# Delta rule in chunks: one TensorE product a level makes the inverse and its factor together, ScalarE copies both out, VectorE turns the factor from that copy

## The chip, the core and the metric

The kernel runs on one core of a Trainium2 chip, in one launch. The metric is the device time of an execution in microseconds (us). The engines are named as in the profile: PE is TensorE's matmul, PEld its weight load, DVE is VectorE, ACT is ScalarE, POOL is GpSimd, SP is SyncE. Each runs its own instructions in program order and waits for the others on semaphores.

## What is computed

The reference chains a gated delta rule, a mixture of experts, a linear attention and a softmax attention. Only the delta rule is touched (4096 tokens, 16 heads of 64):

```
def step(S, inp):
    q_t, k_t, v_t, g_t, b_t = inp
    Sk = einsum('bhkv,bhk->bhv', S, k_t)
    delta = einsum('bhv,bhk->bhkv', v_t, k_t) - einsum('bhv,bhk->bhkv', Sk, k_t)
    S = exp(g_t) * S + b_t * delta
    return (S, einsum('bhkv,bhk->bhv', S, q_t))
```

The kernel takes 64 tokens (a chunk) at once. Inside a chunk the updates depend on each other through a triangular matrix of 64 x 64 per head, which has to be inverted. The inverse is built by doubling: an inverse of blocks of 2, 4, 8, 16, 32 and at last 64.

## The kernel before

All 16 heads are worked on at once, as 8 pairs of heads side by side over 128 partitions; a tile of the phase (`W`) is 128 x 512, and a product over all heads is 16 `te.matmul` calls, which the trace shows as 32 matmul records. `SAME` products keep a head in its half of the array, `OTHER` products cross over, so that one of each can run side by side.

Two chunks (x = 0 and 1) make a couple, and there are 32 couples. `couples(one)` goes over them in 34 iterations. In each, every engine's `one(post, pre, ahead)` works on three couples: `ahead` gets its keys and the triangular matrix (`keys`, `take_upper` L1204, `minus_eye` L1366, `first_inverse` L1372), `pre` is inverted, and `post` goes through the state (`residual`, `updates`, `new_state`, `new_outputs`, `project`). 31 iterations have both `post` and `pre`. The order of the instructions in each engine is written by hand in `one`, the same in all iterations.

One level of the doubling, for each x, is a loop through three engines:

- TensorE `half`: the transposed inverse (`inv_low`) times the matrix (`upper`), into `pd_pre`.
- VectorE `mask_step` (L1250): `step` = `pd_pre` times a mask.
- TensorE `up`: `step` times `inv`, into `pd_low`, beside a product of `post`, `ahead` or the key rows.
- VectorE `turn_low` (L1259) transposes `pd_low` into `inv_low`; ScalarE `keep_inverse` (L1143) copies it to `inv`, with nobody waiting long for it.

There are five levels. Other instructions that matter below: on VectorE `turn_first` (L1255), `take_updates` (L1239), `take_state` (L1244), `turn_values` (L1219), `take_rows` (L1211). On ScalarE `grown` (L1122), `related` (L1127), `keep_values` (L1135, eight pieces of 32 x 256 per chunk), `keep_last_inverse` (L1149), `keep_outputs` (L1154). On GpSimd `decays` (L1334 and L1336), `grow_keys` (L1343), `grow_queries` (L1350), `decay_state` (L1355), `scale_rel` (L1361). ScalarE's `grown(pre, 1)` overwrites what `decay_state(post, 1)` on GpSimd reads, and so waits for it (`sdec_d`); `decay_state(post, 1)` reads the state that VectorE's `take_state(post, 0)` writes.

Lines 1796 to 2012 belong to the second norm phase, which the change doesn't touch. L852 is the line of the helper `product`, through which every 64 x 64 product goes.

## Time and profile before

| | us |
|---|---|
| median of 3 runs | 4261.81 (4256.46 to 4264.55) |
| profiled execution, its own time | 4283.9 |
| its span, first to last instruction | 4282.1 |
| delta phase, first key product to last projection | 541.3 to 1780.0 |
| PE busy | 3885.2 (91%) |
| DVE busy | 3064.9 (72%) |
| ACT busy | 2237.7 (52%) |
| POOL busy | 1036.7 (24%) |

The busy shares are over the whole program. The delta phase is 1239 us of it, and only there does the change act. Durations are those of single instructions; a matmul's end is modelled.

### The profile page before, as it was taken

Reading aid. Unit: us, or ns where it says so; the run is one execution under the profiler, and the core shown is the slowest. Engines: PE = TensorE matmul, PEld = TensorE weight load, DVE = VectorE, ACT = ScalarE, POOL = GpSimd, SP = SyncE. Lnnn points to the kernel's source line nnn. Section 1 sums busy time; section 2 is a strip of 40 time slices with the busy share of each in tenths; the row PEclk is TensorE's granted clock in tenths of the full one; section 3 lists DMA queues with packets and bytes.
Section 4 is the critical chain, followed back from the end, with each engine's and each line's share of the span. In section 5 each row is a group of like instructions: output and inputs, shape, how many; then the busy total and the mean of one; then the engine's idle time right before and its main releaser. Section 6 shows DMA issues by size and latency. Waiting matters only on the chain. (4 is left out here: it accounts for less than half of the span.)

```text
span 4282.1 us, 127123 instructions
## 1 busy us (share of the span) xinstructions
PE 3885.2 (91%) x51725; PEld 2324.9 (54%) x51725; DVE 3064.9 (72%) x5127; ACT 2237.7 (52%) x3389; POOL 1036.7 (24%) x1042
## 2 busy tenths in 40 slices
PE   5999778888888888897887999999999999999998
PEld 4444367777778777675663344444444444444443
DVE  5799856555555555444896787878878787878786
ACT  2788734444444444233442565656656565656564
POOL 1000055555555555102777000000000000000000
PEclk9999999999999999998896999999999999999999
DMA  3544432222222222224345000000000000000000
GB/s 126 183 124 124 142 116 81 84 79 89 85 83 79 85 82 83 75 86 142 106 110 121 8 5 19 5 8 15 10 15 10 13 5 20 5 20 3 10 15 10
DMA packets 271801, 265.25 MB, mean 62 GB/s; under 512 B 53760, under 2 KB 232064, under 8 KB 270496
## 3 DMA queue, kind: packets, MB, share of 16 engines
q1 hardware_dynamic: 250768, 226.07, 17.7%
q0 software_dynamic: 6144, 16.79, 1.2%
q10 hardware_dynamic: 14352, 14.55, 1.0%
q8 instruction: 420, 6.88, 0.7%
q14 instruction: 117, 0.96, 0.1%
HBM read 151.95 MB, written 105.38 MB: 60 GB/s over the span
## 5 line engine op out<-in xcount | busy, mean ns | idle before, releaser
L2418 DVE TENSOR_REDUCE part_max<-p_m 128x1 f32<-128x512 f32 x2118 | 1363.9, 686 | 378.1 <-PE p_m L2260 370.7
L2400 ACT ACTIVATE prob<-p_s 128x1024 f32<-128x1024 f32 x1024 | 1048.6, 1024 | 747.6 <-PE p_s L2324 745.6
L2279 PE MATMUL p_o<-prob,v_one 128*64 128x512 f32 x4096 | 1054.3, 592 | 3.9 <-ACT prob L2400 0.5
L2260 PE MATMUL p_m<-keys,queries 96*64 96x512 f16 x4236 | 661.4, 387 | 28.1 <-DMA keys<-parts_d 20.5
L2324 PE MATMUL p_s<-queries,keys 97*64 97x512 f16 x4096 | 619.0, 380 | 0.0
L2324 PEld LDWEIGHTS p_s<-queries,keys 97*64 97x64 f16 x4096 | 228.1, 109 | 598.4 <-issue 593.3
L2228 POOL TENSOR_TENSOR attn<-o_num,o_inv 32x512 f32<-32x512 f32 x64 | 81.2, 1268 | 1451.6 <-DVE o_inv L2437 1445.2
L852 PE MATMUL pd_pre<-inv_low,upper 64*64 64x64 f32 x10240 | 374.2, 222 | 45.3 <-issue 33.5
L2260 PEld LDWEIGHTS p_m<-keys,queries 96*64 96x64 f16 x4236 | 238.7, 108 | 311.1 <-DVE part_max L2418 56.5
L852 PE MATMUL pd_low<-inv,step 64*64 64x64 f32 x8192 | 365.1, 237 | 45.6 <-issue 42.2
L1143 ACT ACTIVATE inv<-pd_low 128x512 f32<-128x512 f32 x192 | 114.7, 598 | 519.1 <-DVE inv_low L1259 518.7
L2279 PEld LDWEIGHTS p_o<-prob,v_one 128*64 128x64 f32 x4096 | 287.7, 136 | 162.7 <-issue 15.9
L852 PEld LDWEIGHTS pd_pre<-inv_low,upper 64*64 64x64 f32 x10240 | 341.0, 137 | 59.9 <-issue 43.5
L852 PEld LDWEIGHTS pd_low<-inv,step 64*64 64x64 f32 x8192 | 326.9, 145 | 72.4 <-issue 69.9
L588 PE MATMUL p_proj<-xn_t_all,proj_w_sb 128*128 128x512 f32 x768 | 337.7, 596 | 7.7 <-PEq L2563 7.7
L1259 DVE STREAM_TRANSPOSE inv_low<-pd_low 128x512 f32<-128x512 f32 x256 | 183.2, 716 | 217.8 <-PE pd_low L852 214.9
L1250 DVE TENSOR_TENSOR step<-pd_pre,const 128x512 f32<-128x512 f32 x320 | 220.0, 688 | 94.0 <-PE pd_pre L852 73.5
L588 PEld LDWEIGHTS p_proj<-xn_t_all,proj_w_sb 128*128 128x128 f32 x768 | 146.8, 191 | 192.9 <-issue 187.7
L1135 ACT ACTIVATE v_row<-v_turned 32x256 f32<-32x256 f32 x512 | 211.9, 414 | 26.0 <-DVE v_turned L1219 19.1
L852 PE MATMUL pd_kq<-kq_t 64*64 64x128 f32 x2048 | 144.5, 295 | 35.1 <-DMA kq_t<-q_d 31.5
L852 PEld LDWEIGHTS pd_kq<-kq_t 64*64 64x64 f32 x2048 | 128.4, 148 | 37.2 <-issue 36.9
L2437 DVE RECIPROCAL o_inv<-o_raw 128x64 f32<-128x64 f32 x256 | 138.1, 542 | 0.0
(236 smaller groups left out, 5777.7 us busy)
## 6 DMA issues: line engine op xcount, KB each, us to landing
q_d<-conv_q SPq DMA_DIRECT2D x16, 1024.0 KB, 5.0
v_d<-conv_v SPq DMA_DIRECT2D x16, 1024.0 KB, 5.0
k_d<-conv_k SPq DMA_DIRECT2D x16, 1024.0 KB, 6.5
sums<-sums_d SPq DMA_DIRECT2D x128, 128.0 KB, 3.1
kq_t<-k_d SPq DMA_DIRECT2D x32, 512.0 KB, 3.7
kq_t<-q_d SPq DMA_DIRECT2D x32, 512.0 KB, 4.8
sums_k<-sums_d SPq DMA_DIRECT2D x128, 128.0 KB
v_t<-v_d SPq DMA_DIRECT2D x32, 512.0 KB
```

What stands on the lines that cost most here:

```text
L588: last = te.matmul(p_proj[u % RING][:], g.proj_w_sb[:, n, c, p * P:(p + 1) * P], g.xn_t[:, c, b * BLK:(b + 1) * BLK], start=c == 0, stop=c ...
L852: return te.matmul(out[half_of(h if to == SAME else 1 - h), p, :], lhs(p, half_of(h)), rhs(p, half_of(h)), start=start, stop=stop, skip_gr ...
L1135: last = a.activation(v_row[to_p, x, :, to_t], v_turned[from_p, :, from_t], ACT.Copy)
L1143: a.activation(inv_half[x][:] if k == NL - 1 else inv[x][:], p_low[x][:], ACT.Copy).then_inc(up_d[x], 1)
L1250: v.tensor_tensor(step[x][:], p_pre[x][:], over_pairs(masks[:, k - 1, :]), ALU.mult).then_inc(step_d[x], 1)
L1259: v.transpose(inv_low[x][:], p_low[x][:]).then_inc(lowc_d[x], 1)
L2260: last = te.matmul(p_m[k % 2][x * HALF:(x + 1) * HALF, :], queries[0:ROW, p, hh, at:at + HALF], keys[0:ROW, 2 * p + hh, kb * BLK:(kb + 1) ...
L2279: product = te.matmul(p_o[64 * hh:64 * hh + VW, :], g.v_one[:, j, p, hh:hh + 2, :].rearrange("p a d -> p (a d)"), prob[:, j % 2, hh, :], s ...
L2324: last = te.matmul(p_s[j % 2][x * HALF:(x + 1) * HALF, hh, :], keys[0:KR, 2 * p + hh, at:at + HALF], queries[0:KR, p, hh, :], start=True, ...
L2400: a.activation(prob[:, j % 2], p_s[j % 2][:], ACT.Exp, scale=SCORE_SCALE).then_inc(exp_d, 1)
L2418: v.tensor_reduce(part_max[:, hh * SUB + sub, kb:kb + 1], p_m[k % 2][:], AX.X, ALU.max).then_inc(red_d, 1)
L2437: v.reciprocal(o_inv[:, i * PW:(i + 1) * PW], o_raw[:, i * PW:(i + 1) * PW]).then_inc(inv_d, 1)
```

## The change

The matrix `upper` stays, but it is used once. `start_factor` multiplies the first transposed inverse with it: the result is a factor that already has the inverse in it. From there each level has one product of 128 columns: `step` times `both`, where `both` holds the factor in columns 0 to 63 and the inverse in columns 64 to 127 of each pair. ScalarE copies the 128 x 1024 result to SBUF (`keep_both`). VectorE transposes the factor half from that copy (`turn`) and masks the transposed tile (`mask`), which gives the next `step`. At the last level the masking is two small ScalarE copies into a tile with ones on its diagonal (`keep_half`, `last_step`). The key rows of x = 1 go through `pd_u` and into the next iteration, the products of `post` are put beside the long ones (each short product in the first half of a long one), and the order on every engine is written anew.

```diff
     p_both = [ps(f"pd_both{x}", 2) for x in range(2)]
...
+        def start_factor(n, x):
+            return lambda p, h: te.matmul(p_both[x][half_of(h), p, 0:C], inv_low[x][half_of(h), p, :], upper[x][half_of(h), p, :],
+                                          start=True, stop=True)
...
+        def double(n, x, k):
+            if k < NL:
+                return lambda p, h: te.matmul(p_both[x][half_of(h), p, :], step[x][half_of(h), p, :], both[x][half_of(h), p, :], start=True, stop=True)
+            return lambda p, h: te.matmul(p_both[x][half_of(h), p, C:2 * C], step_last[x][half_of(h), p, :], inv_half[x][half_of(h), p, :],
+                                          start=True, stop=True)
...
+        def together(post, pre, ahead):
+            wait_residual(post, 0, pre)
+            wait_old(post, 0, pre)
+            old, res = side_by_side(old_outputs(post, 0), residual(post, 0))
...
+            starts(pre, 0)
+            wait_updates(post, 0)
+            over_heads(updates(post, 0)).then_inc(w_d, 1)
+            starts(pre, 1)
+            doubles(pre, 0, 1)
...
+            made, turned_keys = long_beside_short(double(pre, 1, 1), key_rows(post, 1))
...
+            made, new = long_beside_short(double(pre, 0, 2), new_state(post, 0))
...
+            made, out = long_beside_short(double(pre, 1, 2), new_outputs(post, 0))
...
+            made, res = long_beside_short(double(pre, 0, 3), residual(post, 1))
...
+            made, turned_keys = long_beside_short(double(pre, 1, 3), key_rows(pre, 0))
...
+            over_heads(updates(post, 1)).then_inc(w_d, 1)
+            doubles(pre, 0, 4)
...
+            old, new = side_by_side(old_outputs(post, 1), new_state(post, 1))
...
+            made, out = long_beside_short(double(pre, 1, 4), new_outputs(post, 1))
...
+            for x in range(2):
+                wait_double(pre, x, NL)
...
+                    keyed, made = long_beside_short(keys(ahead, x), double(pre, x, NL))
...
+                project(post, range(x * NPAIR // 2, (x + 1) * NPAIR // 2))
...
+        def keep_factor(n, x):
+            act.wait_ge(upmm_d[x], n.made[1])
+            a.activation(both[x][:, :, 0:C], p_both[x][:, :, 0:C], ACT.Copy).then_inc(up_d[x], 1)
+
+        def keep_both(n, x, k):
+            act.wait_ge(upmm_d[x], n.made[k + 1])
+            a.activation(both[x][:], p_both[x][:], ACT.Copy).then_inc(up_d[x], 1)
+
+        def keep_half(n, x):
+            act.wait_ge(turn_d[x], n.level[NL])
+            a.activation(inv_half[x][:], p_both[x][:, :, C:2 * C], ACT.Copy).then_inc(up_d[x], 1)
+
+        def last_step(n, x):
+            act.wait_ge(turn_d[x], n.level[NL])
+            for h in range(2):
+                last = a.activation(step_last[x][h * C + B32:(h + 1) * C, :, 0:B32], turned[x][h * C:h * C + B32, :, B32:C], ACT.Copy, scale=-1.0)
+            last.then_inc(last_d[x], 1)
...
+                v.transpose(turned[x][:], both[x][:, :, 0:C]).then_inc(turn_d[x], 1)
...
+        def mask(n, x, k):
+            dve.wait_ge(turn_d[x], n.level[k])
+            v.tensor_tensor(step[x][:], turned[x][:], over_pairs(masks[:, k - 1, :]), ALU.mult).then_inc(step_d[x], 1)
```

What stands where. The first place is VectorE's order from the first residual of an iteration to `take_state(post, 0)` (tile `state`), in the kernel before; `step0` and `step1` are the masks of x = 0 and 1:

```order
L1225 TENSOR_TENSOR resid<-v_row,pd_kq 128x512 [waits d_res,d_val0,d_w]
L1250 TENSOR_TENSOR step0<-pd_pre0,const 128x512 [waits d_half0,d_upmm0]
L1250 TENSOR_TENSOR step1<-pd_pre1,const 128x512 [waits d_half1,d_upmm1]
L1239 TENSOR_TENSOR u<-pd_u,beta 128x512 [waits d_w,d_o,d_new]
L1259 STREAM_TRANSPOSE inv_low0<-pd_low0 128x512 [waits d_upmm0]
L1259 STREAM_TRANSPOSE inv_low1<-pd_low1 128x512 [waits d_upmm1]
L1244 TENSOR_TENSOR state<-state_dec,pd_kq 128x512 [waits d_new,d_sdec]
```

`state` stands directly behind level 1 here, and no mask reads a tile that VectorE has just written. The same place in the changed kernel (`turned` is the transposed factor):

```order
L1264 TENSOR_TENSOR resid<-v_row,pd_kq 128x512 [waits d_res,d_val0,d_w]
L1288 STREAM_TRANSPOSE inv_low1<-both1 128x512 [waits d_inv11,d_upmm1]
L1295 STREAM_TRANSPOSE turned0<-both0 128x512 [waits d_up0,d_last0]
L1302 TENSOR_TENSOR step0<-turned0,const 128x512 [waits d_turn0]
L1278 TENSOR_TENSOR u<-pd_u,beta 128x512 [waits d_w,d_o,d_new]
L1295 STREAM_TRANSPOSE turned1<-both1 128x512 [waits d_up1,d_last1]
L1302 TENSOR_TENSOR step1<-turned1,const 128x512 [waits d_turn1]
L1295 STREAM_TRANSPOSE turned0<-both0 128x512 [waits d_up0]
L1302 TENSOR_TENSOR step0<-turned0,const 128x512 [waits d_turn0]
L1295 STREAM_TRANSPOSE turned1<-both1 128x512 [waits d_up1]
L1302 TENSOR_TENSOR step1<-turned1,const 128x512 [waits d_turn1]
L1283 TENSOR_TENSOR state<-state_dec,pd_kq 128x512 [waits d_new,d_sdec]
```

`state` now comes after the masks of level 2, which stood behind it before, and every mask reads two SBUF tiles, `turned` and the constant, and waits for the transposition just ahead of it.

The second place is ScalarE's order around `grow`, the tile of `grown`, before:

```order
L1143 ACTIVATE inv0<-pd_low0 128x512 [waits d_lowc0,d_upmm0]
L1143 ACTIVATE inv1<-pd_low1 128x512 [waits d_lowc1,d_upmm1]
L1127 ACTIVATE rel<-rel 128x8x64 [waits d_min1]
L1122 ACTIVATE grow<-sums_k 128x8x64 [waits d_qg1,d_sums_k_in1,d_kg1,d_sdec]
L1143 ACTIVATE inv0<-pd_low0 128x512 [waits d_lowc0,d_upmm0]
L1143 ACTIVATE inv1<-pd_low1 128x512 [waits d_lowc1,d_upmm1]
```

The copy to `inv0` here is one that no VectorE instruction waits for. In the changed kernel the same place reads:

```order
L1165 ACTIVATE both0<-pd_both0 128x8x64 [waits d_upmm0]
L1146 ACTIVATE grow<-sums_k 128x8x64 [waits d_qg0,d_sums_k_in1,d_kg0,d_sdec]
L1165 ACTIVATE both1<-pd_both1 128x8x64 [waits d_upmm1]
L1151 ACTIVATE rel<-rel 128x8x64 [waits d_min0]
L1169 ACTIVATE both0<-pd_both0 128x1024 [waits d_upmm0]
L1169 ACTIVATE both1<-pd_both1 128x1024 [waits d_upmm1]
L1146 ACTIVATE grow<-sums_k 128x8x64 [waits d_qg1,d_sums_k_in1,d_kg1,d_sdec]
L1169 ACTIVATE both0<-pd_both0 128x1024 [waits d_upmm0]
```

`grow` of x = 1 (the row that waits for `d_qg1`) still stands directly ahead of the copy of level 2 for x = 0. ScalarE's copy is now what VectorE's next transposition waits for.

The third place is GpSimd in the changed kernel, from the last `first_inverse` of an iteration to the second `decay_state` (tile `state_dec`) of the next:

```order
L1414 TENSOR_TENSOR both1<-upper1,const 128x8x64 [waits d_minus1,d_upmm1]
L1397 TENSOR_TENSOR state_dec<-state,grow 128x512 [waits d_state,d_grow0]
L1376 TENSOR_TENSOR rel<-sums,cum 128x8x64 [waits d_rows0,d_sums_in0,d_relb0,d_att0]
L1378 TENSOR_TENSOR rel<-rel,const 128x8x64 [waits d_diff0]
L1385 TENSOR_TENSOR k_g<-kq_t,grow 128x512 [waits d_k_in1,d_grow0,d_res]
L1404 TENSOR_TENSOR upper0<-rel,beta 128x512 [waits d_rel0,d_inv10,d_upmm0]
L1397 TENSOR_TENSOR state_dec<-state,grow 128x512 [waits d_state,d_grow1]
```

The two passes of `decays` (tile `rel`), `grow_keys` (`k_g`) and `scale_rel` (`upper0`) follow one another here, while VectorE is at level 1.

## Rows read from the trace of the kernel before

**Rows 1.** Delta phase: busy PE, PEld, DVE, ACT, POOL (records), clock, DMA, GB/s

```profile
617.50:1757.30 1139.80, 975.02 (x33060) 890.20 (x33058) 665.68 (x1015) 489.99 (x988) 599.12 (x562) 0.96 0.25 81
1152.10:1187.60 35.50, 31.79 (x1112) 28.68 (x1115) 22.25 (x34) 16.38 (x34) 20.32 (x20) 1.00 0.28 89
```

**Rows 2.** What TensorE's products (L852) waited for, 617.5 to 1757.3 us

```profile
  issue: 144.6, 221
```

**Rows 3.** The page's part 3, the queue with TensorE's instructions

```profile
q8 instruction: 420, 6.88, 0.7%
```

**Rows 4.** VectorE by form, 617.5 to 1757.3 us: busy us, mean ns | idle

```profile
L1250 DVE TENSOR_TENSOR step<-pd_pre,const 128x512 f32<-128x512 f32 x300 | 206.3, 688 | 84.3 <-PE pd_pre L852 64.1 <-remote 13.0
...
L1255 DVE STREAM_TRANSPOSE inv_low<-inv 128x512 f32<-128x512 f32 x59 | 41.4, 701 | 0.0
...
L1244 DVE TENSOR_TENSOR state<-state_dec,pd_kq 128x512 f32<-128x512 f32 x60 | 40.1, 669 | 61.1 <-PE pd_kq L852 55.5 <-remote 5.6
```

**Rows 5.** ScalarE by form, same stretch

```profile
L1135 ACT ACTIVATE v_row<-v_turned 32x256 f32<-32x256 f32 x480 | 198.7, 414 | 24.4 <-DVE v_turned L1219 17.9
L1143 ACT ACTIVATE inv<-pd_low 128x512 f32<-128x512 f32 x180 | 107.6, 598 | 494.3 <-DVE inv_low L1259 493.9
L1122 ACT ACTIVATE grow<-sums_k 128x512 f32<-128x512 f32 x60 | 37.9, 632 | 19.3 <-POOL state_dec L1355 18.5
```

**Rows 6.** ScalarE in the page's part 5: the nearest copy of 1024 columns

```profile
L2400 ACT ACTIVATE prob<-p_s 128x1024 f32<-128x1024 f32 x1024 | 1048.6, 1024 | 747.6 <-PE p_s L2324 745.6
```

**Rows 7.** GpSimd by form, same stretch as group 4

```profile
L1372 POOL TENSOR_TENSOR inv<-upper,const 128x512 f32<-128x512 f32 x59 | 75.2, 1275 | 31.1 <-PE pd_low L852 26.8
...
L1336 POOL TENSOR_TENSOR rel<-rel,const 128x512 f32<-128x512 f32 x58 | 68.6, 1183 | 4.5
L1355 POOL TENSOR_TENSOR state_dec<-state,grow 128x512 f32<-128x512 f32 x61 | 64.7, 1060 | 150.0 <-DVE state L1244 150.0
L1334 POOL TENSOR_TENSOR rel<-sums,cum 128x512 f32<-128x512 f32 x58 | 60.6, 1045 | 0.0
```

**Rows 8.** TensorE's timeline: one product of 128 columns alone

```profile
546.48 1.96 PE L852 MATMUL pd_kq<-kq_t 64*64 64x128 f32 x32 [1.47 <-DVE qk L1233]
```

**Rows 9.** TensorE's timeline: one product of 64 columns alone

```profile
1168.84 1.10 PE L852 MATMUL pd_pre<-inv_low,upper 64*64 64x64 f32 x32
```

**Rows 10.** VectorE's timeline, 2104.4 to 2106 us, second norm

```profile
2104.42 0.42 DVE L2012 SCALAR_TENSOR_TENSOR k_feat<-k_pre,k_min 128x256 f32<-128x256 f32 x1
...
2105.82 0.61 DVE L1965 TENSOR_TENSOR x<-x_tile,attn_tok 128x256 f32<-128x256 f32 x1
```

**Rows 11.** GpSimd's timeline, the same stretch

```profile
2104.48 0.94 POOL L1796 TENSOR_TENSOR base<-x,xn 128x256 f32<-128x256 f32 x1
2105.38 0.78 POOL L1802 TENSOR_TENSOR q_feat<-q_max,q_min 128x256 f32<-128x256 f32 x1
```

**Rows 12.** L1965 over the program: min/median/max ns

```profile
L1965 DVE TENSOR_TENSOR x<-x_tile,attn_tok x32: 410/611/617, 2017.5 to 2273.1; 128x256 f32<-128x256 f32 x32
```

**Rows 13.** VectorE's timeline at 2107.7 us

```profile
2107.79 0.43 DVE L1971 BATCH_NORM_STATS2 s_stats<-x 128x6 f32<-128x256 f32 x1
2108.32 0.18 DVE L1973 BATCH_NORM_AGGREGATE s_mean_var<-s_stats 128x2 f32<-128x6 f32 x1
2108.43 0.42 DVE L2027 TENSOR_TENSOR kv_sum<-kv_sum,ps_sum 128x258 f32<-128x258 f32 x1
```

**Rows 14.** VectorE's timeline at 1162 us

```profile
1162.06 0.65 DVE L1244 TENSOR_TENSOR state<-state_dec,pd_kq 128x512 f32<-128x512 f32 x1
```

**Rows 15.** GpSimd's timeline, 1162 to 1164 us

```profile
1162.86 1.06 POOL L1355 TENSOR_TENSOR state_dec<-state,grow 128x512 f32<-128x512 f32 x1 [4.04 <-DVE state L1244]
```

**Rows 16.** ScalarE's timeline, 1162 to 1164 us

```profile
1163.95 0.64 ACT L1122 ACTIVATE grow<-sums_k 128x512 f32<-128x512 f32 x1 [0.60 <-POOL state_dec L1355]
```

**Rows 17.** Two stretches in a row, around a drop of the granted clock

```profile
1381.99:1385.40 3.41, 0.55 (x21) 0.41 (x16) 0.69 (x1) 0.00 (x0) 1.73 (x2) 1.00 0.14 54
1385.40:1388.81 3.41, 3.41 (x82) 3.41 (x85) 1.16 (x2) 0.00 (x0) 0.00 (x0) 0.50 0.03 5
```

More of the change, by code:

```diff
@@ L1097, in one @@
[L1097 to L1106 removed]
+                wait_updates(n, x)
@@ L1108, in _, with one @@
+        def one(post, pre, ahead):
+            if pre is None and post is None:
+                for x in range(2):
+                    wait_keys(ahead, x)
+                    over_heads(keys(ahead, x)).then_inc(kq_d[x], 1)
+            elif post is None:
+                inverse_alone(pre, ahead)
+            elif pre is None:
+                state_alone(post)
+            else:
+                together(post, pre, ahead)
         pe.wait_ge(g.const_in, 16)
@@ L1161, in one @@
             if pre is not None:
-                for x in range(2):
-                    keep_inverse(pre, x, 1)
+                keep_both(pre, 0, 1)
+                keep_both(pre, 1, 1)
+                grown(pre, 1)
+                keep_both(pre, 0, 2)
+            if post is not None:
+                keep_outputs(post, 0)
+            if pre is not None:
+                keep_both(pre, 1, 2)
+                keep_both(pre, 0, 3)
+                keep_both(pre, 1, 3)
             if ahead is not None:
@@ L1166, in one @@
             if pre is not None:
-                grown(pre, 1)
-                for x in range(2):
-                    keep_inverse(pre, x, 2)
-            if post is not None:
-                keep_outputs(post, 0)
-            if pre is not None:
-                keep_inverse(pre, 0, 3)
+                keep_half(pre, 0)
+                last_step(pre, 0)
             if post is not None:
@@ L1188, in one @@
             if pre is not None:
-                for x in range(2):
-                    keep_last_inverse(pre, x)
+                keep_values(pre, 1, 1)
         couples(one)
@@ L1285, in one @@
             if pre is not None:
-                mask_step(pre, 1, 3)
+                turn(pre, 1, 4)
+                mask(pre, 1, 4)
+                turn(pre, 0, 5)
             if post is not None:
@@ L1387, in one @@
             if ahead is not None:
-                for x in range(2):
-                    decays(ahead, x)
+                decays(ahead, 0)
+            if pre is not None:
+                grow_keys(pre, 0)
+            if ahead is not None:
                 scale_rel(ahead, 0)
```

380 lines of the change are left out of this document (174 added, 206 removed).

## Prediction

> **What bounds the kernel now.** I first cut the delta phase into iterations, from one copy to `attn_tok` to the next. From 617.5 to 1757.3 us there are 30 of them in 1139.8 us, so 38.0 us each, at a mean granted clock of 0.96; one that ran at 1.00 took 35.5 us. In it TensorE was busy for 31.79 us and VectorE for 22.25 [rows 1]. TensorE has 33060 records in the 30 iterations, 1102 each, which are the 34 products of 32 records plus 16 of the projection. So it is TensorE, first of all, that sets the end.
>
> Then what TensorE waited for: 144.6 us in 221 idle times carry no releaser at all ("issue"), 4.8 us an iteration [rows 2]. They lie inside products, one per 150 records. The queue that carries the instructions brought 6.88 MB in 420 packets over the program [rows 3]. I read these two together as TensorE running ahead of its own instructions: 1104 matmuls an iteration come barely fast enough. That is a reading; no row says it outright. Next to it VectorE's masks waited 84.3 us for `pd_pre` and the others, 2.8 us an iteration [rows 4], and ScalarE's copies of the inverse had 494.3 us to spare [rows 5]. So before, ScalarE is off the path, and the loop VectorE - TensorE has little slack.
>
> The profiled execution took 4283.9 us, 22.1 us (0.5%) above the median. I make the sum against it and carry the difference to the median.
>
> **What the change takes away.** Eight products an iteration: 26 times 32 records plus 16 are 848 instead of 1104, 23% fewer. The "issue" time of 4.8 us should shrink to well under 1 us, since the instructions arrive with a quarter to spare. The columns hardly shrink: a product of 128 columns took 1.96 us where one of 64 took 1.10 [rows 8, 9], and the short ones stand beside long ones as they did before.
>
> **What it adds.** A level was: product, mask .69, product, transposition .70. It now is: product, ScalarE copy, transposition, mask. So the copy comes onto the path. I know it for 512 columns, .60 [rows 5], and for 1024, 1.02 [rows 6]. With two x in turn each level has 1.96 + 1.02 + .70 + .69 plus three handoffs. For a handoff between engines I take .1: `state` ended at 1162.71 and `decay_state` began at 1162.86, it ended at 1163.92 and `grown` began at 1163.95 [rows 14 to 16]. The mask waits for the transposition on its own engine; one such wait on VectorE cost .10 (an end at 2108.22, a start at 2108.32), where an unwaited instruction began .08 before the end of the one ahead (2108.50 to 2108.43) [rows 13].
>
> The Trainium skill, in "VectorE: DVE Perf Modes", section "The DRAIN you can't avoid", says that a semaphore between chained VectorE instructions costs nothing extra. By it the five masks on the path would give back 5 x .18 = .9 us an iteration, 28 us in all; the trace has .10 against -.08, and the sum goes by the trace.
>
> **The iteration after, step by step.** t = 0 is where ScalarE starts the first copy of an iteration, `keep_factor(pre, 0)`; all at full clock.
>
> (A) The copy .60, .1, transposition .70, .10: the first mask could start at 1.50. GpSimd counts from the end V of `turn_values(1)`, 4.43 before t = 0 (below): transposition for `take_upper` .69, .1, `minus_eye` 1.28, .1, `first_inverse` 1.28, `decay_state` 1.06, `decays` 1.05, .1 and 1.18 [rows 7], so the second pass of `decays` is in flight from V+5.66 to V+6.84, and the mask is ready at V+5.93. Does it have to wait? In the second norm phase L1965 took .41 at least, and .61 when GpSimd's two-input `q_feat` was in flight, ending .27 to .28 after it (2106.16 to 2106.43); and GpSimd's `base` at 2104.48 took .94, behind VectorE's `k_feat` [rows 10 to 12]. Now that the mask reads two SBUF tiles and no longer PSUM, it does the same: it ends .55 (512 columns instead of 256) after GpSimd, at V+7.39 = 2.96, where it would end at 2.19. Price .77.
>
> (B) `take_updates` .69, transposition .70, .1: 4.45. GpSimd's `grow_keys`, held until 2.96, takes 1.18 and `scale_rel` 1.05, until 5.19, so the mask of x = 1 ends at 5.74 instead of 5.14. Price .60.
>
> The Trainium skill has this as a rule, in "SBUF — State Buffer", section "Who interferes with whom": a VectorE instruction with two SBUF inputs and a GpSimd instruction use one pair of ports, and whoever has it keeps the other out for its whole length. It speaks against this change, and .61 against .41 agrees; without it the sum below would be 1.37 x 31 = 42 us lower.
>
> (C) .1, `double(1,1)` 1.96, .1, copy 1.02, .1, transposition .70, .1, mask .69: 10.41. That is the mask of level 2 for x = 1, and `take_state(post, 0)` stands behind it (the first pair of orders).
>
> (D) `take_state` .67, .1, `decay_state` 1.06, .1, `grown` .63 and then the copy for `double(0,2)` 1.02, since this stands behind `grown` on ScalarE (the second pair of orders): 3.58, to 13.99. Without this wait the copy would be done some 3 us earlier; `state` was not late before, since `take_state` stood ahead of level 2.
>
> (E) .1, .70, .1, .69, .1, `double(0,3)` 1.96, .1, copy 1.02, .1, .70, .1, .69: 20.35.
>
> (F) TensorE is in turn behind itself: .1, `double(0,4)` 1.8, the old outputs and the new state .9, `double(1,4)` 1.96: 25.11.
>
> (G) .1, transposition .72, .1, `keep_half` .60, `last_step` .83 (two pieces at .414): 27.46. Then ScalarE alone: four pieces of `keep_values` 1.66, `keep_inverse` .60, four pieces 1.66: 31.38; .1, `turn_values(1)` .68, since there is one `v_turned`: V = 32.16. .1, 1.66, .60, the `attn_tok` copy .41, 1.66: the next t = 0 at 36.59, with .414 from the 480 pieces [rows 5].
>
> So 36.6 us at full clock, 35.2 without the contention. It compares with 35.5 at full clock before.
>
> **The clock.** Before an iteration lost 38.0 - 35.5 at its 0.96. What a fall looks like: after 3.41 us in which TensorE was busy for .55, the next 3.41 us had a clock of 0.50 (1.2 instead of 2.4 GHz) [rows 17]. After the change TensorE is idle for about 2.1 us ahead of `double(0,1)` (A) and 3.2 us ahead of `double(0,3)` (D), each iteration, and the chain runs through the products behind them. One such stretch can cost up to half of it, 1.7, and two 3.4; a chain that has copies and masks in the stretch loses less. I take 1.1 each, 2.2; bounds 0 and 3.4. What is left of the pauses: .4, bounds 0 and 1.
>
> Sum: 36.6 + 2.2 + .4 = 39.2 to 39.3, 1.3 more than 38.0. Times 31 iterations with both: +40. The three others have no `post` or no `pre` and wait on each copy alone: five levels with .3 to .6 more each, +3. 4283.9 + 43 = 4327, and 22 less on the median: **4305 us**.
>
> Low end: 36.6 minus half the contention (.7), no clock loss, .2 of pauses: 36.1, 4261.8 - 1.9 x 31 + 3 = 4206. High end: 36.6 + 3.4 + 1, and another mask (D or E) that meets GpSimd at +.7: 41.7, 4261.8 + 3.7 x 31 + 3 = 4379.
>
> **Rivals.**
> Faster: TensorE's instructions were the bound, as the 4.8 us of "issue" say, and the gaps of the new chain don't bring the clock down. The period is then the chain's, 36.6: 4261.8 - 1.4 x 31 + 3 = 4221. For it: 35.5 at full clock before contains those 4.8 us. Against: the chain is longer than what TensorE needs, and its idle times are longer than before. It decides where clock and pauses together are under 1.3 us an iteration. Chance .27.
>
> No change within what can be told: the wait in (D) is covered, because `scale_rel` and `decay_state` come earlier than I count, or the masks hardly wait; the chain is then near 35.2, plus 2.6 are 37.8: 4261.8 - .2 x 31 + 3 = 4259. That the change does nothing at all is in the same case. Chance .11.
>
> Slower by more: more masks meet GpSimd, and the clock takes its whole 3.4: 41 us and over, 4350 and up. For it: the masks of every level now have the form that waits. Against: after `scale_rel` GpSimd has only `decay_state` and the grown tiles left. Chance .20.
>
> My forecast, 38.4 to 40.5 us, on its own 4277 to 4340: chance .42.
>
> 0.2% (8.5 us) is about what a measurement of this kernel can tell from no change. Faster .27, same .11, slower .62. The range of 4205 to 4355 leaves out some .13 above and .06 below.
>
> **What would show it.** In the profile after: the distance of two `attn_tok` copies (39.3, against 38.0), and 848 records in it; "issue" of TensorE under 1 us an iteration; L1302's mean over .69, with single ones at 1.2 to 1.5 at level 1, which end .55 after a GpSimd instruction; L1169 at 1.02; ScalarE idle at L1146, released by `state_dec`, some 2 to 3 us an iteration, and TensorE idle for the same time ahead of `double(0,3)`, with a drop of the granted clock behind it. The forecast is wrong if masks stay at .69, if ScalarE isn't idle at `grow`, or if the clock stays at 0.96 or above in spite of the idle times; and it is wrong the other way if `issue` stays at 4 us.

## The result, and the profile after

| | before | after |
|---|---|---|
| median of the timed runs, us | 4260.19 (4256.46 to 4264.55, 5 runs) | 4282.17 (4274.60 to 4284.42, 5 runs) |
| ratio after to before | | 1.0048, 95% interval 1.0033 to 1.0062 |
| the same again, in a later session | 4284.04 (17 runs) | 4304.31 (5 runs) |
| ratio | | 1.0042, 95% interval 1.0029 to 1.0055 |

The change makes the kernel slower by 0.45%, some 20 us. The forecast was slower, 4305 us (+45): the sign is right, the size is twice too large. The kernel before took 4260 to 4284 us in the sessions of this study; so every kernel below is given as a ratio to the runs of the kernel before that stand beside it, and 0.1% is 4.3 us.

The page's first lines of the kernel after:

```profile
span 4281.2 us, 110710 instructions
...
PE 3829.6 (89%) x43533; PEld 2266.3 (53%) x43533; DVE 3125.1 (73%) x5127; ACT 2401.8 (56%) x3581; POOL 1068.3 (25%) x1044
...
PEclk9999989999999999998897999999999999999999
```

PE was busy for 3885.2 us in the kernel before and is for 3829.6 us now. Columns of the next rows are as in [rows 1]: a stretch, its length, busy time of PE, PEld, DVE, ACT and POOL with the number of records, granted clock, DMA share and GB/s. The 30 iterations, one without a drop of the clock, and one with:

```profile
626.20:1756.90 1130.70, 913.78 (x25403) 831.35 (x25395) 721.07 (x1016) 645.64 (x1169) 627.57 (x562) 0.96 0.24 80
1154.10:1190.20 36.10, 28.98 (x863) 26.33 (x859) 23.67 (x34) 21.68 (x41) 21.23 (x20) 1.00 0.28 87
1227.90:1265.90 38.00, 30.87 (x869) 28.22 (x865) 23.97 (x34) 21.56 (x41) 21.27 (x20) 0.96 0.25 83
```

An iteration takes 1130.7 / 30 = 37.7 us, against 38.0 in [rows 1], and 36.1 at a clock of 1.00. The records are 847 an iteration, as counted. PE is busy 913.78 us instead of 975.02. So these two profiled executions are equally long (4283.9 and 4283.1 us) though the medians are some 20 us apart: the 30 iterations are 9 us shorter, and the start is longer by nearly as much. The first `attn_tok` copy was at 617.5 before, after first keys at 541.3, 76.2 us. Now it is

```profile
542.99 0.48 PE L855 MATMUL pd_kq<-kq_t 64*64 64x128 f32 x2 [30.32 <-DMA kq_t<-q_d]
```

```profile
626.22 0.38 ACT L1227 ACTIVATE attn_tok<-pd_u 128x256 f32<-128x256 f32 x1
```

83.2 us. That is 7 us in the iterations that fill the pipeline, where, as the prediction had it, each level waits on the copy alone.

What TensorE waited for in the 30 iterations (line, releaser, us in total, times, longest):

```profile
PE pd_both L917 <- DVE step L1302: 106.4, 66, 2.9
PE pd_both L917 <- issue: 69.0, 86, 1.6
PE pd_o L855 <- DVE upper L1243: 25.2, 23, 1.5
PE pd_kq L855 <- issue: 5.9, 9, 0.9
```

Where [rows 2] had 144.6 us of "issue", there are 80 us of "issue" now, and 131.6 us of waiting for VectorE. But most of the 80 us is a wait for VectorE too, under another name. TensorE's two starts at level 1 read

```profile
1159.05 1.96 PE L917 MATMUL pd_both<-both,step 64*64 64x128 f32 x32 [1.56 <-issue]
1161.65 0.29 PE L917 MATMUL pd_both<-both,step 64*64 64x128 f32 x1 [0.64 <-issue]
```

and each stands .11 us behind the end of one of VectorE's masks (1158.94 and 1161.54, shown below). In the 30 iterations 69 of the 80 us end like this, within .2 us behind an instruction of VectorE. The other 11 us, .4 an iteration, are left of the 4.8 that the kernel before had. VectorE and ScalarE by form (busy us, mean ns | idle, releaser):

```profile
L1302 DVE TENSOR_TENSOR step<-turned,const 128x512 f32<-128x512 f32 x240 | 217.1, 905 | 8.3
L1295 DVE STREAM_TRANSPOSE turned<-both 128x512 f32<-128x512 f32 x240 | 169.8, 708 | 197.8 <-ACT both L1169 169.3 <-ACT both L1165 28.5
```

```profile
L1169 ACT ACTIVATE both<-pd_both 128x1024 f32<-128x1024 f32 x180 | 183.8, 1021 | 234.2 <-PE pd_both L917 234.2
...
L1146 ACT ACTIVATE grow<-sums_k 128x512 f32<-128x512 f32 x60 | 37.8, 631 | 99.8 <-POOL state_dec L1397 99.1
```

A mask took 688 ns in [rows 4] and takes 905 now. ScalarE stood 18.5 us at `grow` for `state_dec` before [rows 5] and stands 99.1 us there now, 3.3 an iteration. The predicted waits are there. Three places show them singly. Level 1, VectorE and GpSimd of the iteration that begins at 1154.1 (start, us, instruction):

```profile
1156.90 0.71 DVE L1295 STREAM_TRANSPOSE turned<-both 128x512 f32<-128x512 f32 x1 [0.95 <-ACT both L1165]
1157.64 1.30 DVE L1302 TENSOR_TENSOR step<-turned,const 128x512 f32<-128x512 f32 x1
...
1160.20 1.34 DVE L1302 TENSOR_TENSOR step<-turned,const 128x512 f32<-128x512 f32 x1
```

```profile
1157.23 1.17 POOL L1378 TENSOR_TENSOR rel<-rel,const 128x512 f32<-128x512 f32 x1
...
1159.95 1.05 POOL L1404 TENSOR_TENSOR upper<-rel,beta 128x512 f32<-128x512 f32 x1
```

The mask begins at 1157.64, `decays` on GpSimd ends at 1158.40 and the mask at 1158.94: .54 behind it. The second mask ends at 1161.54, again .54 behind `upper` (1161.00). The four masks of levels 2 and 3 take .69, the two of level 4 on average 1.03 and .82. Then ScalarE:

```profile
1167.99 0.63 ACT L1146 ACTIVATE grow<-sums_k 128x512 f32<-128x512 f32 x1 [3.30 <-POOL state_dec L1397]
1168.53 1.01 ACT L1169 ACTIVATE both<-pd_both 128x1024 f32<-128x1024 f32 x1
```

`double(0,2)` is long done; its copy begins behind `grow`. And TensorE with its clock, in an iteration with a drop:

```profile
1244.87 0.32 PE L917 MATMUL pd_both<-both,step 64*64 64x128 f32 x1 [2.87 <-DVE step L1302]
```

```profile
1241.90:1244.80 2.90, 0.10 (x2) 0.00 (x0) 1.39 (x3) 2.84 (x4) 1.00 (x1) 1.00 0.22 76
1245.10:1248.50 3.40, 3.40 (x82) 3.40 (x78) 2.36 (x4) 0.08 (x1) 1.30 (x2) 0.50 0.70 226
```

TensorE is idle for 2.87 us, and behind that the granted clock is 0.50 for 3.4 us, the lower of its two levels (1.2 instead of 2.4 GHz). There are 25 such drops in the 30 iterations. All begin 16.2 to 18.1 us into the iteration, at the end of the idle time ahead of `double(0,3)` or just behind it; that idle time is 2.8 us on average. The idle time ahead of `double(0,1)`, the 1.5 us shown above, is followed by none.

### The profile page after: what moved, and what is told of

Read it like the earlier page. It is cut to its first block and busy times, and to the rows that moved or that the text cites. A ratio compares the mean times of both kernels' runs of the same rounds, so it can differ in the third digit from the quotient of the medians.

```text
span 4281.2 us, 110710 instructions
## 1 busy us (share of the span) xinstructions
PE 3829.6 (89%) x43533; PEld 2266.3 (53%) x43533; DVE 3125.1 (73%) x5127; ACT 2401.8 (56%) x3581; POOL 1068.3 (25%) x1044
## 5 line engine op out<-in xcount | busy, mean ns | idle before, releaser
L917 PE MATMUL pd_both<-both,step 64*64 64x128 f32 x8192 | 542.0, 287 | 185.0 <-DVE step L1302 113.5
L917 PEld LDWEIGHTS pd_both<-both,step 64*64 64x64 f32 x8192 | 491.3, 143 | 222.6 <-DVE step L1302 137.6
L1169 ACT ACTIVATE both<-pd_both 128x1024 f32<-128x1024 f32 x192 | 196.0, 1021 | 251.4 <-PE pd_both L917 251.4
L1295 DVE STREAM_TRANSPOSE turned<-both 128x512 f32<-128x512 f32 x256 | 181.2, 708 | 209.4 <-ACT both L1169 179.5
L1302 DVE TENSOR_TENSOR step<-turned,const 128x512 f32<-128x512 f32 x256 | 233.2, 911 | 8.9
L855 PEld LDWEIGHTS pd_kq<-kq_t 64*64 64x64 f32 x2048 | 119.6, 135 | 47.6 <-issue 45.9
L657 DVE SCALAR_TENSOR_TENSOR conv_k<-raw,conv_w_sb,conv_k 128x2048 f32<-128x2048 f32 x48 | 112.2, 2351 | 23.7 <-ACT raw L631 22.6
L980 PE MATMUL pd_u<-wo,o_t 128*128 128x256 f32 x512 | 127.3, 392 | 0.8 <-ACT o_t L1190 0.8
```

The lines of the kernel that those rows point to most:

```text
L855: return te.matmul(out[half_of(h if to == SAME else 1 - h), p, :], lhs(p, half_of(h)), rhs(p, half_of(h)), start=start, stop=stop, skip_gr ...
L917: return lambda p, h: te.matmul(p_both[x][half_of(h), p, :], step[x][half_of(h), p, :], both[x][half_of(h), p, :], start=True, stop=True)
L1169: a.activation(both[x][:], p_both[x][:], ACT.Copy).then_inc(up_d[x], 1)
L1295: v.transpose(turned[x][:], both[x][:, :, 0:C]).then_inc(turn_d[x], 1)
L1302: v.tensor_tensor(step[x][:], turned[x][:], over_pairs(masks[:, k - 1, :]), ALU.mult).then_inc(step_d[x], 1)
```

## The experiments

All ratios are to the kernel before, run beside them.

| kernel | ratio | 95% interval |
|---|---|---|
| before_again | 0.9994 | 0.9981 to 1.0007 |
| before_fewer | 0.9828 | 0.9815 to 0.9841 |
| before_no_scatter | 1.0002 | 0.9992 to 1.0012 |
| after (first, again) | 1.0048, 1.0042 | 1.0033 to 1.0062, 1.0029 to 1.0055 |
| after_fewer | 1.0070 | 1.0055 to 1.0084 |
| after_no_scatter | 1.0004 | 0.9993 to 1.0014 |
| after_early | 1.0014 | 1.0005 to 1.0023 |
| filler | 1.0052 | 1.0039 to 1.0066 |
| filler_early | 0.9961 | 0.9948 to 0.9974 |
| grow_later | 0.9876 | 0.9861 to 0.9891 |
| mask_psum | 0.9903 | 0.9888 to 0.9919 |
| **mask_first** | **0.9711** | 0.9698 to 0.9725 |
| mask_first_grow_later | 0.9716 | 0.9703 to 0.9730 |
| mask_first_early | 0.9744 | 0.9731 to 0.9756 |

**Is the profile of before typical?** The kernel before, unchanged.

> The kernel before, unchanged, profiled a second time. Its first profiled execution took 4283.9 us, 24 us above the median of its timed runs, and its 30 iterations from one attn_tok copy to the next took 38.0 us each. Theory 1, that this profile was an unlucky one: a second profile lies near 4260 us and its iterations take some 0.7 us less, 37.2 to 37.3. Theory 2, that taking a profile adds the time: the second profile is near 4284 us again with 38.0 us an iteration, as the changed kernel's profile would then have to be above its own median too, which it is not by more than 2 us.

```profile
616.50:1742.90 1126.40, 946.63 (x33064) 866.78 (x33068) 665.17 (x1016) 490.21 (x989) 599.04 (x562) 0.98 0.25 81
```

An iteration took 37.5 us, at a mean clock of 0.98, and the profiled execution 4267.9 us. The first profile had 23 drops of the clock in its 30 iterations, this one 14; 9 drops are 13 us, 1.5 each. Its iterations lie between what the two theories said (37.2 to 37.3, and 38.0), nearer to theory 1: the number of drops differs between executions of the same kernel, and the 38.0 us from which I started were some .2 too many for the average of the two.

**The instructions of before.** In `over_heads`, the second product of four pairs is cut to its last matmul, so the outputs are not computed (`short` is set in the four calls):

```diff
+                        if one_product is not None and not (short and i == 1 and (p, h) != (NPAIR - 1, 1)):
```

> The kernel before, with four of the short products of an iteration that run side by side with a product of the inverse (both key_rows, both new_outputs) left out but for their last matmul: 124 matmuls fewer of 1104, the outputs are not computed. Every wait, every other instruction and the products beside them stay. Theory 1, that the delivery of instructions bounds TensorE in the kernel before (144.6 us of idle time without a releaser in 30 iterations): 11% fewer instructions take 11% off an iteration until the chain bounds it, some 3 to 4 us, 90 to 125 us in all: 4135 to 4170 us. Theory 2, that the chain of dependences bounds it and the pauses are covered by it: within 20 us of 4260 us.

```profile
615.20:1665.30 1050.10, 925.12 (x29489) 850.81 (x29490) 663.28 (x1016) 489.87 (x988) 598.44 (x562) 0.99 0.27 87
```

35.0 us an iteration and 1.7% less time, with 983 records instead of 1102. The products beside them, and all that the other engines wait for, are the same. So matmuls that stand beside others cost time all the same: 11% fewer gave 7% of an iteration. That is theory 1, a little below its numbers. Against before_again TensorE is busy for 21.5 us less in the 30 iterations and idle for 54.8 us less, so the larger part of what was won is idle time. That this idle time is a wait for instructions can be read from the traces. In before_again 120 pauses without a releaser are over .3 us and inside a product, 134 us in all. 116 of them (131 us) end 1.15 to 1.65 us after a packet of 16 KB has landed on the instructions' queue; pauses at random would do so in 12% of cases. In the first profile 88 of 140 do, 97 of 116 us, and of the other 52 all but 3 stand beside GpSimd's indirect DMAs (more of these below). The same cut in the changed kernel:

> The changed kernel with the same four short products left out but for their last matmul as in the run before_fewer (both key_rows, both new_outputs), 124 matmuls fewer of 848; the outputs are not computed. In the kernel before this took 78 us off. Theory 1, that the changed kernel is bound by its chain and not by the delivery of instructions: within 15 us of 4282 us. Theory 2, that instructions still bound it (81 us of idle time without a releaser are left in 30 iterations, of 146): 1.5 to 2.5 us an iteration, 45 to 78 us off.

It gave nothing, as theory 1 has it; the time was even 0.2% longer than the changed kernel's. The count of instructions no longer bounds.

**The contention.** The second operand of every mask is taken from PSUM, so the constant masks are left out:

```diff
-            v.tensor_tensor(step[x][:], turned[x][:], over_pairs(masks[:, k - 1, :]), ALU.mult).then_inc(step_d[x], 1)
+            v.tensor_tensor(step[x][:], turned[x][:], p_both[x][:, :, 0:C], ALU.mult).then_inc(step_d[x], 1)
```

> The changed kernel with the constant masks left out: the second operand of every mask instruction is pd_both in PSUM instead of the constant in SBUF, same size, same waits. The inverses are not computed rightly, the instructions are the same in number. Theory 1, that a mask with two SBUF inputs waits for GpSimd (mean 0.905 us now, 1.32 at level 1 for both x): the mean of L1302 falls to about 0.69, the chain loses 0.63 + 0.63 us at level 1 and some tenths elsewhere, and with 1.3 us x 31 the time falls by 40 us, to about 4242 us. Theory 2, that the waits at level 1 are given back by the wait for state_dec or by TensorE: the mean falls but the time by less than 10 us.

```profile
L1302 DVE TENSOR_TENSOR step<-turned,pd_both 128x512 f32<-128x512 f32 x240 | 165.0, 687 | 8.3
```

```profile
622.90:1703.30 1080.40, 903.84 (x25399) 822.17 (x25390) 670.63 (x1016) 646.29 (x1169) 601.69 (x562) 0.97 0.26 84
```

Every mask takes .687, and the iteration 36.0 us instead of 37.7: 8 masks at .218 less are 1.74, and 1.67 arrived. The kernel is 1.4% below the changed one, some 60 us where theory 1 had 40. Not all of that is the contention itself, for this profile has 17 drops of the clock and the changed kernel's had 25. Like compared with like, the iterations with a drop went from 38.0 to 36.6 us on average, those without from 36.1 to 35.3 (34.9 at the least). So the contention is on the path, with .8 to 1.4 us of its 1.74, which is about the 1.37 of the forecast; the rest is that fewer iterations had a drop, and whether the masks brought that about no run shows.

**The wait for `state_dec`.** On ScalarE:

```diff
-                grown(pre, 1)
                 keep_both(pre, 0, 2)
...
                 keep_both(pre, 1, 2)
+                grown(pre, 1)
```

> The changed kernel with grown(pre, 1) on ScalarE moved behind the copies of level 2, nothing else. Theory 1, that ScalarE's wait for state_dec is on the path (in the trace of the changed kernel double(0,2) is done near 1240.0 and its copy begins at 1242.33, behind grown): the chain shortens by 2.3 us an iteration, and TensorE's idle time ahead of double(0,3) shrinks from 2.9 to about 0.6 us, so that the drop of the clock behind it (2.0 us in 26 of 30 iterations) goes too. That is 2.3 x 31 = 71 us at least and 3.9 x 31 = 121 us at most: 4160 to 4211 us. Theory 2, that TensorE and the masks of x = 1 take its place: under 0.5 us an iteration, 4267 to 4282 us.

```profile
620.50:1684.20 1063.70, 884.62 (x25399) 794.00 (x25389) 746.37 (x1016) 654.88 (x1170) 634.28 (x562) 1.00 0.26 85
```

```profile
PE pd_both L917 <- issue: 69.6, 89, 1.6
PE pd_both L917 <- DVE step L1302: 58.3, 73, 1.5
```

35.5 us an iteration and no drop of the clock among the 30; 1.7% below the changed kernel, 72 us. Theory 1 by its total, the lower end of it. Its parts are otherwise than written: half of the iterations take 35.2 us or less where the changed kernel's without a drop took 36.1, so the chain got shorter by .9 and not by 2.3 (the masks of level 3 meet GpSimd now: 1.16 and 1.33 us, where they took .69), and the rest is the clock.

**Is it the clock?** `double(1,2)` is computed twice, in the idle time that brings the clock down:

```diff
             made, out = long_beside_short(double(pre, 1, 2), new_outputs(post, 0))
-            made.then_inc(upmm_d[1], 1)
             out.then_inc(o_d, 1)
+            over_heads(double(pre, 1, 2)).then_inc(upmm_d[1], 1)
```

> The changed kernel with one product more in each iteration: double(1,2) is computed a second time, to the same place from the same tiles, in TensorE's idle time ahead of double(0,3) (2.9 us, in which ScalarE's copy of double(1,2) has to stand behind grown and the copy of x = 0 anyway). 32 matmuls more, nothing less. Theory 1, that TensorE's idle time is what brings the granted clock down behind it, in 26 of 30 iterations, at 2.0 us each: the drops go and with them 1.7 us an iteration, 52 us: near 4230 us, at a period of 36.1. Theory 2, that the clock falls whatever TensorE does there: the time stays at 4282 us or rises by up to 10 us.

```profile
622.30:1762.20 1139.90, 956.77 (x26363) 859.55 (x26354) 712.00 (x1016) 649.69 (x1170) 627.68 (x562) 1.00 0.24 80
1230.30:1268.10 37.80, 31.88 (x896) 28.70 (x891) 23.66 (x34) 21.63 (x41) 21.27 (x20) 1.00 0.25 83
```

The drops are gone (clock 1.00, none in 30 iterations), as theory 1 has it: TensorE's idle time is what precedes them. But the time did not fall. An iteration takes 37.8 us at full clock, where the changed kernel has 36.1. I had not expected this, in either theory. Something else takes the 1.7 us:

```profile
1254.03 0.34 PE L855 MATMUL pd_o<-q_g,state 64*64 64x64 f32 x4
1254.51 0.21 PE L855 MATMUL pd_kq<-u,k_row 64*64 64x64 f32 x1
...
1255.22 0.21 PE L855 MATMUL pd_kq<-u,k_row 64*64 64x64 f32 x1 [0.37 <-issue]
...
1255.97 0.21 PE L855 MATMUL pd_o<-q_g,state 64*64 64x64 f32 x1 [0.38 <-issue]
...
1256.69 0.29 PE L917 MATMUL pd_both<-both,step 64*64 64x128 f32 x1
```

```profile
1253.22 1.00 POOL L1423 DMA_INDIRECT slots_d<-rows,place  x1 [0.28 <-POOL place L1420]
1254.53 0.97 POOL L1423 DMA_INDIRECT slots_d<-rows,place  x1 [0.30 <-issue]
```

Inside a pair of products TensorE stops three times, up to .6 us from one matmul to the next, without a releaser, and once more ahead of the next product; 1.9 us in all. It does so beside the scatter in every iteration, while GpSimd issues its two indirect DMAs. These pauses are of another kind than those of the kernel before: of filler's 104 over .3 us inside products, only 16 end 1.15 to 1.65 us after a packet of instructions. In the changed kernel's first profile there is one pause of .46 to .50 in its place, in the iterations with a drop of the clock and also in its five without one.

**Is it the scatter?** It is moved on GpSimd from behind `decays(ahead, 1)` to ahead of `grow_keys(pre, 1)`:

```diff
                 grow_queries(pre, 0)
+            if post is not None:
+                scatter(post)
...
                 decays(ahead, 1)
-            if post is not None:
-                scatter(post)
```

> filler (double(1,2) computed twice, no drops of the clock, 37.8 us an iteration nevertheless) with the scatter moved as in after_early. Theory 1, the scatter's DMAs cause the cluster of pauses at 23.8 to 26.4: the cluster goes from there, TensorE is idle at 15 to 17 us anyway, and the iteration comes to the 36.1 us that the changed kernel's undisturbed iterations take, 50 us below filler. Theory 2, the cluster comes from the number of instructions in the stretch ahead of it (256 matmuls from 17 to 26 us): it stays where it is and the period stays at 37.8.

```profile
622.60:1737.30 1114.70, 952.12 (x26363) 855.32 (x26355) 711.37 (x1016) 651.04 (x1169) 644.97 (x562) 1.00 0.25 82
```

0.9% below filler (39 us), two thirds of the iterations at 36.1 to 37.1, and the cluster at 24 to 26 us is gone (one pause of .46 is left there). Theory 1 by its place, but not in full by its number: the mean is 37.2 and not 36.1, and other pauses stand behind the old place now, at 28 and 36 us. The changed kernel itself, again and with the move:

> The changed kernel unchanged, profiled and timed again beside the three below. The first time it was 1.0048 of the kernel before, with 25 drops of the clock in 30 iterations of 37.69 us. If that was typical: 1.003 to 1.007, 20 to 27 drops, 37.6 to 37.8 us.

> The changed kernel with GpSimd's scatter(post), two indirect DMAs, moved from behind decays(ahead, 1) to ahead of grow_keys(pre, 1), into GpSimd's idle time 15 to 19 us after the start of an iteration. Theory 1, that the scatter's DMAs hold up TensorE's instructions (in the run filler TensorE pauses four times, 1.9 us, between 23.8 and 26.4 us of every iteration, just where the scatter's 96 packets run from 24.5 to 26.3): in this kernel that pause is .49 only, behind a drop of the clock, so little is won: 0 to 0.5 us an iteration, 0 to 15 us. Theory 2, that the clock is what costs here and nothing else: no change against after_again.

after_again had the cluster (.59 and .60 us among it) in all eight of its iterations without a drop, which took 37.8 to 38.1 us; with 23 drops it took 38.6 us an iteration. Ratio and drops were as guessed, but the first profile, at 37.7, was one with little of the cluster, and the guess of 37.6 to 37.8 missed. Cluster and drop add up in part: a drop alone made an iteration 1.9 us longer than 36.1 (38.0, first profile), the cluster alone 1.7 (37.8), and the iterations of after_again with a drop took 38.9 on average, 2.8 more. after_early is 0.3% below after_again, and has no cluster. The 30 iterations of after_again:

```profile
623.10:1782.30 1159.20, 931.43 (x25399) 839.63 (x25391) 726.99 (x1016) 645.84 (x1170) 627.72 (x562) 0.96 0.24 78
```

Then the scatter's DMAs replaced by two tiny copies, before and after:

```diff
-                po.indirect_dma_start(g.slots_d[:, :], bass.IndirectOffsetOnAxis(ap=place[:, n.odd, k:k + 1], axis=0),
-                                      rows[:, n.odd, :], None).then_inc(scattered[n.odd], 16)
+                po.tensor_copy(place[:, n.odd, k:k + 1], g.slot[:, n.c, k:k + 1]).then_inc(scattered[n.odd], 16)
```

> The kernel before with GpSimd's two indirect DMAs of an iteration replaced by two tiny copies (the tokens' rows are not scattered, the expert stage reads what is in memory). Theory 1, that the scatter's DMAs pause TensorE: a cluster of about 1.5 to 2 us at 22 to 24 us goes from each iteration, and the time falls by 30 to 60 us (ratio 0.986 to 0.993). Theory 2, that pauses follow from the number of instructions alone, and only fall where the scatter happens to be: under 10 us (ratio above 0.998).

> The changed kernel with the same replacement. Theory 1: the undisturbed iterations take 36.1 us and no longer 37.8 (as 8 of 30 did in the run after_again), the others keep their drop of the clock; 12 to 40 us less than the changed kernel, ratio 0.995 to 1.001 to the kernel before. Theory 2: ratio 1.003 to 1.006, as it was.

After: 0.4% below the changed kernel, theory 1; the pauses of .6 are not in its iterations, and the two without a drop take 36.0 and 36.3 us. Before: no difference at all (1.0002), theory 2; its pauses are at all places of an iteration and stay, and 116 of the 121 over .3 us inside products end 1.15 to 1.65 us after a packet of instructions. So the two kernels are held up in two ways, and without the scatter they are equal (1.0002 and 1.0004). The cluster comes and goes between executions of one kernel: the first profile of the kernel before has it in most iterations, before_again has not. after_fewer has the same cluster at the same place as filler in its undisturbed iterations of 37.8 us. That may be what kept fewer instructions from helping it; after_fewer without the scatter was not run.

**A better order of the same work.** VectorE masks first, out of PSUM and with the transposed mask, and then transposes; ScalarE's copy waits for the mask and runs beside the transposition. No instruction more or less (VectorE's order in `one` is changed to match, and the wait for the last level's copy moves to the mask):

```diff
-        doublings.append((... * (s[:, None] % (2 * w) >= w) * (t[None, :] % (2 * w) < w) + ...
+        doublings.append((... * (s[:, None] % (2 * w) < w) * (t[None, :] % (2 * w) >= w) + ...
...
         def keep_both(n, x, k):
-            act.wait_ge(upmm_d[x], n.made[k + 1])
+            act.wait_ge(turn_d[x], n.level[k + 1])
...
-                v.transpose(turned[x][:], both[x][:, :, 0:C]).then_inc(turn_d[x], 1)
+                v.transpose(step[x][:], turned[x][:]).then_inc(step_d[x], 1)
...
-            v.tensor_tensor(step[x][:], turned[x][:], over_pairs(masks[:, k - 1, :]), ALU.mult).then_inc(step_d[x], 1)
+            v.tensor_tensor(turned[x][:], p_both[x][:, :, 0:C], over_pairs(masks[:, k - 1, :]), ALU.mult).then_inc(turn_d[x], 1)
```

> The changed kernel with VectorE's two steps of a level exchanged: it masks first, out of pd_both in PSUM with the transposed mask, and then transposes the masked tile; ScalarE's copy waits for the mask and runs beside the transposition. Same instructions in number and size. Theory 1, that copy, contention and order are on the path: the masks fall to 0.69 (one SBUF input), a level takes 0.69 + max(1.02, 0.70) in place of 1.02 + 0.70 + 0.69, 0.8 us less in levels 2 to 4 and 0.6 at level 1, and the 1.3 us of contention at level 1 go: some 5 us of 37.7 less, the wait behind grown still there: 4130 to 4160 us. Theory 2, that the wait for state_dec swallows what is won ahead of it: 2 us less an iteration, about 4220 us.

```profile
616.20:1617.20 1001.00, 888.08 (x25403) 806.39 (x25393) 669.53 (x1016) 641.35 (x1169) 603.97 (x562) 1.00 0.27 91
```

```profile
L1302 DVE TENSOR_TENSOR turned<-pd_both,const 128x512 f32<-128x512 f32 x240 | 163.5, 681 | 37.9 <-PE pd_both L917 36.5 <-PE pd_both L903 0.9
```

2.9% below the kernel before, 3.3% below the changed one: 33.4 us an iteration, masks at .681, one drop of the clock. It is the fastest kernel of the study, and theory 1 by its number. Three things come together in it: the masks read PSUM, which alone gave 1.4% (mask_psum); the copy runs beside the transposition; and the drops of the clock are gone, as they are in grow_later. No run separates the last two. With grow_later:

> mask_first together with grow_later (grown(pre, 1) behind the copies of level 2). Theory 1, the two add up until TensorE bounds: it was busy for 29 us an iteration at full clock, and with 1 to 2 us of pauses the period comes to 31 to 32 us, 4282 - 6 x 31 = 4080 to 4110 us. Theory 2, that ScalarE's tail of 16 pieces of keep_values and VectorE's turn_values behind it bound an iteration once the levels are short: 33.5 to 34.5 us, 4150 to 4180 us.

Nothing more (0.9716), as theory 2 has it. In mask_first ScalarE still stands 52.4 us at `grow` for `state_dec`, here not at all, and an iteration takes 33.4 us in both, so this wait is no longer what comes last; the shortest iterations take 32.6 and 32.2 us. That the tail of `keep_values` bounds them was not tested by itself. With the scatter moved:

> mask_first (4152 us, 32.6 us an iteration in the undisturbed ones, with three pauses of 0.6, 0.6 and 0.4 us at 19 to 21 us, where its scatter runs) with the scatter moved ahead of grow_keys(pre, 1). Theory 1, the scatter's DMAs hold up TensorE's instructions: the cluster goes and 0.5 to 1.2 us an iteration with it, 4115 to 4137 us. Theory 2, pauses only move to another place: within 8 us of 4152.

0.3% slower, which neither theory had. The cluster of pauses (.41, .62, .56 us) went with the scatter, from 19 to 21 us of the iteration to 13 to 15 us, where TensorE has more to do. Its profile has 8 drops of the clock where mask_first's has 1, so how much of the 0.3% is the cluster's place stays open.

## Why the prediction was right in sign and twice too large

- **What bounds before.** I read the 144.6 us of "issue" with the instructions' queue as a delivery that comes barely fast enough. before_fewer bears it out, and so does the time from the landing of an instruction packet to the end of a pause. The change took it away: .4 us an iteration were left in the first profile, as forecast, although the profile's own "issue" says 2.7. The 35.5 us at full clock that I compared with was one of the shortest iterations: the 12 without a drop in that profile took 35.0 to 38.9, 36.8 on average.
- **The chain of 36.6 us.** 36.1 was measured at full clock, with the pauses in it. The terms of step (C) add up to 4.77 and not to 4.67, so the chain as written is 36.7. From the first `keep_factor` at 1156.20, the mask of step (A) ended at 2.74 (I had 2.96), (B) at 5.34 (5.74), the copy of (D) at 13.34 (13.99). The order of the steps held in each; but most of the handoffs that I took at .1 were .03 to .04 (a copy ended at 1162.08, the transposition began at 1162.11). Nine of them lie on the path to (D), which is most of the .65 there.
- **The wait on the own engine.** I priced the mask behind its transposition at .10, by one instruction of another kind [rows 13]. The transposition at 1164.72 ended at 1165.43 and its mask began at 1165.47, .04 later; `state`, which waits for nothing new, began .08 before the mask's end. So the semaphore costs .12 against free running, and not .18. The Trainium skill's sentence in "VectorE: DVE Perf Modes", section "The DRAIN you can't avoid", that it costs nothing extra, is off by .12 here, my row by .06.

```profile
1164.72 0.71 DVE L1295 STREAM_TRANSPOSE turned<-both 128x512 f32<-128x512 f32 x1 [1.18 <-ACT both L1169]
1165.47 0.69 DVE L1302 TENSOR_TENSOR step<-turned,const 128x512 f32<-128x512 f32 x1
1166.08 0.68 DVE L1283 TENSOR_TENSOR state<-state_dec,pd_kq 128x512 f32<-128x512 f32 x1
```

- **The contention, 1.37 us.** The mechanism, the place and even the .55 behind GpSimd's end were right. The masks got 1.74 us longer, since those of level 4 pay too, and .8 to 1.4 of it was on the path (mask_psum), so the amount was about right. The Trainium skill's rule in "SBUF — State Buffer", section "Who interferes with whom", was the right warning: masks .905 with two SBUF inputs, .687 with one.
- **`grown` ahead of the copy.** Right in mechanism: 3.3 us an iteration, and .9 of it on the chain by itself. The rest of its cost is the clock.
- **The clock, 2.2 us, and the pauses, .4 us.** This is the step that failed. I priced a loss of 1.1 us behind each of two idle stretches, ahead of `double(0,1)` and of `double(0,3)`. Only the second, 2.8 us long, was followed by drops, in 25 of 30 iterations at 1.9 us, which is 1.6 an iteration. The first was 1.5 us long instead of 2.1 and was followed by none. The mean clock stayed at 0.96, which the prediction itself names as a sign that it is wrong. I also added .4 for pauses on top of the chain, where the 36.1 already has them in it. With the chain's .5 these make up the 1.5 us between 39.2 and the 37.7 of the first profile. In the second (38.6) the drops cost less, 1.1 us in 22 iterations, and a cluster of pauses beside the scatter took their place in part. For that I had no term at all; it is worth 0.4% of the time in the changed kernel and nothing in the one before. Why five iterations of the first profile had neither stays open.
- **The base.** The sum went from 38.0 to 39.3 us, in the two profiles of each kernel it is 38.0 and 37.5 before, 37.7 and 38.6 after: +.4 on the mean, 12 us in 30 iterations, and with 7 us of the start 19 us, near the 20 measured. With two profiles of each kernel, .5 and .9 us apart, such a close fit is in part luck. The start I had at 3.
- **The 22 us off for the median** assumed that a profile of the changed kernel lies above its median as the one of before did. It lies within 1 us of it (4283.1 and 4282.2). That assumption took 22 us off where the error was, and made the forecast better than its steps.

Of the rivals, "faster" needed clock and pauses together under 1.3 us an iteration, and they were 1.6 in the first profile (37.7 less 36.1) and 2.5 in the second. "Same" needed a covered wait at (D) or masks that hardly wait, and had neither; without the scatter the two kernels are equal for another reason.

## What to carry to other kernels

Taking instructions off the bounding engine pays only as far as the next chain allows. Here 124 matmuls fewer of 1102 were worth 1.7% in the kernel before; the change took 255 away, and a copy, masks with two SBUF inputs and an order on ScalarE took it all back. When a copy and a transposition must follow a product, ask which reads PSUM first: masking out of PSUM and copying beside the transposition turned the same instructions from 0.45% slower into 2.9% faster.

A drop of the clock and a cluster of pauses are not simply to be added up: alone they cost 1.9 and 1.7 us here, together 2.8. Take one away and look whether the other comes in its place, before either is named the cause. And compare iterations in like state: a profile with fewer drops looks faster for that alone. An idle time that the profile puts down to "issue" is not yet a wait for instructions; look what ended just ahead of it.

## What the runs showed of the hardware that was not expected

- TensorE's delivery of instructions: 124 matmuls fewer, side by side with others, took 1.7% off a kernel in which TensorE had 1102 in 38 us. Of its 120 pauses over .3 us inside products, 116 ended 1.15 to 1.65 us after a 16 KB packet of instructions had landed (before_again).
- A cluster of three or four pauses of .4 to .6 us on TensorE, inside a product, goes with GpSimd's indirect DMAs: it moved with them from 19 to 13 us (mask_first_early), and went with them (after_no_scatter). In the kernel before, taking them out changed nothing. These pauses end at no fixed time after an instruction packet (16 of 104 in the 1.15 to 1.65 us, in filler), unlike those of the kernel before; by which way they hold TensorE up no run here settles.
- A product repeated in TensorE's idle time took all drops of the clock away (25 to 0 in 30 iterations), without a gain in time. An idle time of 2.8 us was followed by a drop in 25 of 30 iterations, one of 1.5 us in none.
